# Cross attention: heads masked in the softmax reciprocals on GpSimd, four heads summed on VectorE, one output product per tile

## What is computed

```python
x = x + L1_xattn(layernorm(x), ctx, ctx, mask, padding, Wq, Wk, Wv, Wo)

def L1_xattn(q, k, v, attn_mask, key_padding_mask, Wq, Wk, Wv, Wo):
    qh = (q @ Wq.T) split in 16 heads of 8;  kh = (k @ Wk.T) ...;  vh = (v @ Wv.T) ...
    qh, kh = apply_rope(qh), apply_rope(kh)
    scores = qh @ kh.T / sqrt(8) + masks
    out = softmax(scores) @ vh        # 257 keys
    return (out with its heads side by side) @ Wo.T
```

## Time and profile before

| | us |
|---|---|
| median of three runs | 2311.27 (2311.0 to 2311.86) |
| profiled execution | 2309.65, of which the span is 2307.9 |
| cross attention, first to last `exp` (L2276) | about 1044.5 to 1655.4 in the span |
| one tile in its steady part (four units) | 19.09 |
| PE, DVE, ACT, POOL busy in such a tile | 18.75, 15.54, 14.75, 11.43 |

### The profile page before, as it was taken

The page is one execution under the profiler, slowest core; times in us unless marked ns, Lnnn a source line. Parts: engine busy times, 40 slices in busy tenths (PEclk is TensorE's granted clock), DMA queues, the critical chain, the costliest instruction groups (busy, mean ns, idle before and its releaser), DMA issues. The chain is left out here.

```text
span 2307.9 us, 81023 instructions
## 1 busy us (share of the span) xinstructions
PE 2119.3 (92%) x27948; PEld 1563.2 (68%) x27949; DVE 1535.6 (67%) x5463; ACT 1300.8 (56%) x3747; POOL 1027.1 (45%) x935
## 2 busy tenths in 40 slices
PE   7989999997999899978999999999889999989994
PEld 4657777774677677756777777777556665665992
DVE  4578888874777743347888888888666666754442
ACT  3555555555888433336777777777645555532330
POOL 1024444333888300006555656555266666625115
PEclk9999999997999899988999999999999999979997
DMA  6640000000000000000111111111140000001112
GB/s 161 174 130 1 0 0 0 0 1 1 1 0 0 1 1 0 0 26 25 36 34 34 34 34 34 34 34 34 35 169 0 0 0 0 0 2 41 42 42 77
DMA packets 41208, 71.52 MB, mean 31 GB/s; under 512 B 6176, under 2 KB 30624, under 8 KB 40480
## 3 DMA queue, kind: packets, MB, share of 16 engines
q1 hardware_dynamic: 37792, 63.55, 9.4%
q0 software_dynamic: 3328, 6.82, 0.9%
HBM read 60.91 MB, written 9.44 MB: 30 GB/s over the span
## 5 line engine op out<-in xcount | busy, mean ns | idle before, releaser
L2276 ACT ACTIVATE xat_scores<-xat_scores,xat_least 128x257 f32<-128x257 f32 x512 | 258.5, 505 | 103.5 <-DVE xat_least L2410 102.3
L2410 DVE CUSTOM_DVE_ANT_0 xat_scores<-bank,xat_mask_b 128x257 f32<-128x257 f32 x512 | 207.6, 422 | 88.7 <-PE bank L2120 87.9
L1050 POOL TENSOR_TENSOR gqa_rnorm<-gqa_norm_min,gqa_minus_half 128x12 f32<-128x12 f32 x64 | 145.8, 2278 | 104.9 <-DVE gqa_norm_min L1127 104.9
L2178 PE MATMUL bank<-ident,xat_scores 128*128 128x128 f32 x1024 | 189.2, 287 | 0.0
L2178 PEld LDWEIGHTS bank<-ident,xat_scores 128*128 128x128 f32 x1024 | 116.4, 142 | 81.0 <-issue 49.0
L690 POOL TENSOR_TENSOR lin_q_softmax<-lin_q_exp,lin_q_rsum 128x512 f32<-128x512 f32 x64 | 66.7, 1042 | 223.2 <-DVE lin_q_rsum L751 223.2
L1693 DVE SCALAR_TENSOR_TENSOR X<-bank,expert_shares,X 128x128 f32 (+1 forms) x256 | 72.0, 343 | 130.9 <-PE bank L1607 130.7
L1630 ACT ACTIVATE moe_gelu<-bank 128x512 f32<-128x512 f32 x128 | 76.5, 597 | 146.1 <-PE bank L1597 146.1
L1607 PEld LDWEIGHTS bank<-moe_w,moe_gelu 128*128 128x128 f32 x1024 | 124.2, 192 | 30.8 <-issue 18.2
L1368 POOL TENSOR_TENSOR bat_scores<-bat_scores,bat_max 128x512 f32<-128x512 f32 x128 | 130.5, 1041 | 32.5 <-DVE bat_max L1400 32.5
L1400 DVE CUSTOM_DVE_ANT_0 bat_scores<-bank,bat_causal_add 128x128 f32<-128x128 f32 x512 | 110.7, 286 | 47.2 <-PE bank L1256 47.2
(11 more groups left out here) (320 smaller groups left out, 5826.9 us busy)
## 6 DMA issues: line engine op xcount, KB each, us to landing
glu_ctx_N<-in_ctxN SPq DMA_DIRECT2D x32, 576.0 KB, 4.3
xat_ctx_T<-in_ctxT SPq DMA_DIRECT2D x32, 516.0 KB, 3.6
xat_pad<-in_xat_pad SPq DMA_DIRECT2D x32, 128.5 KB, 3.4
expert_w<-in_glx_w SPq DMA_DIRECT2D x1, 4096.0 KB, 14.9
slot_rows<-gqa_zero_rows SPq DMA_DIRECT2D x1, 2560.0 KB, 11.0
slt_rows<-slot_rows SPq DMA_DIRECT2D x40, 64.0 KB, 1.8
slot_results<-slt_y POOLq DMA_DIRECT2D x40, 64.0 KB, 1.8
moe_w<-in_moe_w SPq DMA_DIRECT2D x2, 1024.0 KB, 5.8
```

The costliest lines, as they stand in the source:

```text
L1050: pool.tensor_tensor(rn[h][:, :], sm[h][:, :], half_neg[:, :], ALU.pow).then_inc(rnorm, 1)
L2178: m = pe.transpose(dst[:, c * P:(c + 1) * P], sx[j % 2][:, g, c * P:(c + 1) * P], k.ident[:, :])
L2276: act.activation(sx[j % 2][:, g, :], sx[j % 2][:, g, :], ACT.Exp, bias=mn[j % 2][g][:, 0:1], scale=-1.0, accum_out=sm[j % 2][:, g:g + 1]). ...
L2410: dve.tensor_tensor_reduce(sx[j % 2][:, g, :], pS[g][:, 0:J], mb[slot][:, j, :], 1.0, BIG, ALU.add, ALU.min, mn[j % 2][g][:, 0:1]).then_in ...
```

## The change

The head mask moves from the output weights to the reciprocals. A new constant `head_of_row` (128x32) is 1 where a row's head group matches the column's head. GpSimd in place of ACT widens the reciprocals (`spread_r` for `r_copy`) and multiplies them by it, so that the transposed reciprocals are zero at the features that belong to another head. DVE's `o_keep` becomes `o_scale`, of the same shape, written in place; a new DVE instruction per unit, `o_sum`, adds the four head columns, 128x128 to 128x32, into a tile `o` of a quarter of the size. `y` is then one product with the plain weights. GpSimd's run for the next tile is cut in pieces between its four `spread_r`. PE's waits for banks are on the new semaphore `o_scaled`; `y` still waits for `o_kept`, which `o_sum` now raises.

```diff
-        woh = sb("w_out_of_head", [P, QH, P])
-        os_ = [sb(f"o{i}", [P, QH, BT, S]) for i in range(2)]
+        os_ = [sb(f"o{i}", [P, BT, S]) for i in range(2)]
@@ PE, y
-                for h in range(QH):
-                    m = pe.matmul(dst[:, 0:P], os_[slot][:, h, :, :], woh[:, h, :], start=(h == 0), stop=(h == QH - 1))
-                m.then_inc(y_made, 1)
+                pe.matmul(dst[:, 0:P], os_[slot][:, :, :], wo[:, :], start=True, stop=True).then_inc(y_made, 1)
@@ PE, body: waits for a bank
-                    pe.wait_ge(wo_ready, QH)
-                        wait(pe, o_kept, u - 1)
+                        wait(pe, o_scaled, u - 1)
@@ ACT, body
-                    if more:
-                        r_copy(*two)
@@ GpSimd
+            def spread_r(t, slot, j):
+                u = BT * t + j
+                pool.wait_ge(recip, u + 1)
+                wait(pool, no_made, u - 1)
+                pool.tensor_tensor(rw[j % 2][:, :, :], spread(rs[j % 2][:, :], 32),
+                                   hrow[:, :].unsqueeze(1).broadcast_to([P, G, 32]), ALU.mult).then_inc(r_spread, 1)
-                if not last:
-                    read_pad(t + 1, 1 - slot)
-                    keep_mask(t + 1, 1 - slot)
-                    add_mask(t + 1, 1 - slot)
-                    keep_ctx(t + 1, 1 - slot)
-                    rotate_q(t + 1)
-                    spread_q(t + 1, 1 - slot)
+                for j in range(BT):
+                    if not (first and j < 2):
+                        spread_r(*ago(t, slot, j, 2))
+                    if j == 0 and not last:
+                        read_pad(t + 1, 1 - slot)
+                    if j == 1 and not last:
+                        keep_mask(t + 1, 1 - slot)
+                        add_mask(t + 1, 1 - slot)
+                    if j == 2 and not last:
+                        keep_ctx(t + 1, 1 - slot)
+                    if j == 3 and not last:
+                        rotate_q(t + 1)
+                        spread_q(t + 1, 1 - slot)
+                if last:
+                    spread_r(t, slot, 2)
+                    spread_r(t, slot, 3)
@@ DVE
-            def o_keep(t, slot, j, at):
+            def o_scale(t, slot, j, at):
                 u = BT * t + j
                 dve.wait_ge(o_mixed, u + 1)
+                dve.tensor_tensor(om[j % 2][:, :, :], om[j % 2][:, :, :],
+                                  unit_bank(*at)[:, RC].rearrange("p (h q) -> p h q", q=S), ALU.mult).then_inc(o_scaled, 1)
+
+            def o_sum(t, slot, j):
+                u = BT * t + j
+                dve.wait_ge(o_scaled, u + 1)
                 wait(dve, y_made, t - 1)
-                dve.tensor_tensor(os_[slot][:, :, j, :], om[j % 2][:, :, :],
-                                  unit_bank(*at)[:, RC].rearrange("p (h q) -> p h q", q=S), ALU.mult).then_inc(o_kept, 1)
+                dve.tensor_reduce(os_[slot][:, j, :], om[j % 2][:, :, :].rearrange("p h q -> p q h"), AX,
+                                  ALU.add).then_inc(o_kept, 1)
@@ DVE, body
-                    for h in range(QH):
-                        dve.tensor_scalar(woh[:, h, :], wo[:, :], hdiag[:, h:h + 1], None, ALU.mult).then_inc(wo_ready, 1)
                         reciprocal(*one)
+                    if more:
+                        o_sum(*two)
                     if j == 0 and not last:
                         norm(t + 1, 1 - slot)
```

More of the change, by code:

```diff
@@ L2030, in sem @@
             return sems[-1]
-        wq, wqr, wk, wv, wo, qtab, cosk, sink, hdiag, mask = preloaded
-        woh = sb("w_out_of_head", [P, QH, P])
+        wq, wqr, wk, wv, wo, qtab, cosk, sink, hdiag, mask, hrow = preloaded
         nmask = sb("mask_negated", [P, J])
@@ L2061, in stage_cross_attention @@
         VC, PC, LC = slice(0, NC * P), slice(NC * P, (NC + 1) * P), slice((NC + 1) * P, (NC + 1) * P + BT)
[L2063 removed]
+        next_loaded, o_scaled = sem("next_weights_loaded"), sem("o_scaled")
         landed = [sem("ctx_landed0"), sem("ctx_landed1")]
@@ L2196, in body @@
                         if j == 1:
-                            wait(pe, o_kept, u - 2)
+                            wait(pe, o_scaled, u - 2)
                         else:
@@ L2226, in body @@
                     if j == 1 and not last:
-                        wait(pe, o_kept, u - 1)
+                        wait(pe, o_scaled, u - 1)
                         x_transpose(t + 1, 1 - slot, (j, XX))
                     if j == 2 and not last:
-                        wait(pe, o_kept, u - 1)
+                        wait(pe, o_scaled, u - 1)
                         q(t + 1, 1 - slot, (j, XX))
                     if j == 3 and not first:
-                        pe.wait_ge(o_kept, u - 1)
+                        pe.wait_ge(o_scaled, u - 1)
                         y(t - 1, 1 - slot, (j, XX))
@@ L2277, in exp @@
                                accum_out=sm[j % 2][:, g:g + 1]).then_inc(s_exp, 1)
-            def r_copy(t, slot, j):
-                u = BT * t + j
-                act.wait_ge(recip, u + 1)
-                wait(act, no_made, u - 1)
-                act.activation(rw[j % 2][:, :, :], spread(rs[j % 2][:, :], 32), ACT.Copy).then_inc(r_spread, 1)
             def p_copy(t, slot, j):
@@ L2300, in body @@
                 for j in range(BT):
-                    some, more = not (first and j == 0), not (first and j < 2)
-                    one, two = ago(t, slot, j, 1), ago(t, slot, j, 2)
-                    if more:
-                        r_copy(*two)
+                    some = not (first and j == 0)
+                    one = ago(t, slot, j, 1)
                     if some:
@@ L2477, in body @@
                     if more:
-                        o_keep(*two, (j, NO))
+                        o_scale(*two, (j, NO))
                     least(t, slot, j, 3)
@@ L2491, in body @@
                     o_mix(t, slot, 2, (0, NO))
-                    o_keep(t, slot, 2, (0, NO))
+                    o_scale(t, slot, 2, (0, NO))
                     t_copy(t, slot, 3, 3, (0, T3))
                     reciprocal(t, slot, 3)
+                    o_sum(t, slot, 2)
                     aggregate(dve, k, added, 2 * NT - 2, 0, NT - 1)
                     o_mix(t, slot, 3, (0, XX))
-                    o_keep(t, slot, 3, (0, XX))
+                    o_scale(t, slot, 3, (0, XX))
+                    o_sum(t, slot, 3)
                     add(t, (1, T1))
@@ L2537, in build @@
                 ("q_table", [P, 2, 2 * P]), ("cos_k", [P, J]), ("sin_k", [P, J]), ("head_in_group", [P, 4]),
-                ("mask", [P, J]))]
+                ("mask", [P, J]), ("head_of_row", [P, 32]))]
             for_linear = [(lin[0][:, :, :, :], a["lin_wqkv"]), (lin[1][:, :, :], a["lin_wout"]),
@@ L2546, in build @@
             for_cross = [(t[tuple(slice(None) for _ in t.shape)], a["xat_" + n]) for t, n in zip(
-                xat, ("wq", "wq_rot", "wk", "wv", "wo", "q_table", "cos_k", "sin_k", "head_in_group", "mask"))]
+                xat, ("wq", "wq_rot", "wk", "wv", "wo", "q_table", "cos_k", "sin_k", "head_in_group", "mask", "head_of_row"))]
             for_clamped = [(t[tuple(slice(None) for _ in t.shape)], a[n]) for t, n in zip(
@@ L2651, in layouts @@
     o["xat_head_in_group"] = ((row[:, None] % 32) // 8 == np.arange(4)[None]).astype(np.float32)
+    o["xat_head_of_row"] = (row[:, None] // 32 == np.arange(32)[None] // 8).astype(np.float32)
     o["xat_mask"] = np.tile(g["mask_1x1xSxS2_fk0"].reshape(S, J), (4, 1))
```

3 lines of the change are left out of this document (removed).

## The result

The kernel after takes 2289.70 us (median of 4 runs, 2286.35 to 2290.88), the kernel before 2311.14 in the same comparison (2309.11 to 2311.86). The ratio is 0.9911, 95% interval 0.9897 to 0.9924. The forecast was 2288.3, in a range of 2284 to 2300. The profiled execution after took 2290.58 with a span of 2288.1 (before 2309.65 and 2307.9); the mean granted TensorE clock was 0.968 in it, 0.966 before.

What follows compares the result with a forecast made beforehand. PE was taken as the bound, with `y` lengthening each fourth unit. 30 x 0.73 = 21.9 us plus 0.25 and 0.8 gave 22.95 us gained, 2286.7 profiled and 2288.3 as median, range 2284 to 2300.

Steps and rivals of the forecast that it cites:

- The mechanism: End of each tile's fourth unit: eight passes of `y` hold PE 1.08 us and delay the next scores.
- y, 0.73 per tile: Fourth unit on PE: cutting `y` from eight passes to two saves 0.73 us per tile, 5.23 to 4.50.
- the loop that was to take over at 4.50: Scores, DVE's run from first to fourth `least`, then the next scores: 4.50 us a unit with nothing in between.
- o_sum: New DVE reduction in each unit: 0.28 us, hidden in DVE's wait for the scores with 0.21 us slack, cost nothing.
- spread_r: GpSimd's widening of reciprocals: 0.48 us, third unit's ready at S + 1.78 (S: scores' start), wanted at 2.12, cost nothing.
- rival B: Third unit's late `spread_r` stops PE and decides the tile; slower beyond a cost c of 1.0, 2328 at 1.27; chance 0.07.
- Contention: DVE's normalization beside GpSimd's `spread_r` in every second unit: nothing at its median; worst case 1.04 us, 0.19 per tile.
- rival A: `spread_r` at 0.73 us or the normalization's worst case, 6 us each: 2294 for one, 2300 for both; chance 0.13.
- Start and end: Stage's start 0; at its end the last `y` gains 0.8 us and the `y` before it 0.25.
- The total: Whole kernel: 22.95 us gained, profiled execution 2309.65 to 2286.7, median of the runs 1.62 above it, 2288.3.
- C: Scores behind `y` were held by DVE's masks all along, so a shorter `y` gives nothing: 2311; chance 0.03.
- rest of 0.02: Chance left for outcomes beyond the range, beside the rivals of a slower kernel and of no difference.

Runs made afterwards that it cites:

- e1_y_four: The kernel after with its one output product issued four times, so eight passes as before: 2308.56 us, ratio 0.9991 to the kernel before.
- before_y_one: The kernel before with only the first of its four output products (three heads left out), nothing else changed: 2290.04 us, ratio 0.9907.
- spread_x2: The kernel after with one more GpSimd product of the same shape ahead of each `spread_r`: 2292.47 us, ratio 0.9917 to the kernel before.
- spread_x3: The kernel after with two more GpSimd products of the same shape ahead of each `spread_r`, on another chip: ratio 0.9997 to the kernel before.
- e5_before_pe_loop4: The kernel before with PE's loop body written out over four tiles instead of two: 2335.72 us, ratio 1.0104 to the kernel before.
- sum_x3: The kernel after with two more VectorE reductions of the same shape ahead of each `o_sum`: 2392.02 us, ratio 1.0347 to the kernel before.

## Why the prediction was right

**The mechanism.** `y` in the way of the scores, and nothing else: right, by e1_y_four and before_y_one from both sides. That the total came so near is partly luck (below).

**y, 0.73 per tile: the term that was too large.** Two parts of it failed. The step "PE is free at 1310.86 to 1310.92, before the masks allow the next scores" priced two passes at 0.27 to 0.33. Measured from the start of `y` to the start of the scores they hold PE 0.42, which is 0.13 behind the last `least`'s result instead of 0.06, and the fourth unit is 4.57 and not 4.50. A price per pass taken from eight queued ones (1.08 / 8 = 0.135) spreads over all of them the 0.19 us that stays when passes go; with 0.11 a pass and that share, two make 0.42. (The other price, 0.33 from the four passes of `q`, is 0.32 by its own row, and has the same fault.) So PE, and not the masks, still lets the scores go: from eight passes to four and to two the unit fell by the same 0.11 a pass, and the loop that was to take over at 4.50 had not done so. And a unit's end was treated as the same everywhere, while every second one has PE's turn behind `y`: 4.84. From the first scores of the stage to those of its last unit it is 609.05 before and 592.18 after, -16.87 for the forecast -21.9. Of the missing 5.0 the 13 turns at 0.33 short of 0.73 make 4.3, and the other 17 tiles, at 0.07 on average, make 1.2 (0.5 comes back in the other units by hundredths). The warning was in the code and in the trace, though not in the rows shown: PE's body of two tiles, and first units of 4.63 beside 4.50 in the kernel before, where VectorE's first `least` comes 1.57 us behind the scores instead of 1.42.

**o_sum.** Forecast 0.28, recorded 0.345 and 0.26 to 0.27 to the next instruction's start. The slack in the first unit was forecast as 0.21 and stands in the trace as 0.22 away from the turn. Hidden, as said.

**spread_r.** Forecast 0.48 with bounds 0.45 to 0.73; recorded 0.40, 0.36 from start to start, below the lower bound. The reciprocal of the second unit ended at S + 0.37, as forecast. The third unit's product is ready at S + 1.34 instead of 1.78; of the 0.44, two products cheaper than 0.48 make half, and the steps between instructions, priced at about 0.1 each where the record has overlaps, the other half. That leaves 0.78 us of slack for 0.34. The point from which rival B decides was put at c = 1.0; spread_x2 (0.8) costs nothing, and spread_x3 (1.2) lies a little beyond the point.

**Contention.** Median 389 ns and longest 882, for 558 and 1037 before: not worse, as taken, but not for the reason given. The prediction took the duration as a spread. It follows a rule that all fourteen traces of this case show: in 31 of the 32 tiles (25 in e5_before_pe_loop4) the normalization starts while a GpSimd instruction runs, and each time it ends 0.08 to 0.09 us behind that one's end. A GpSimd instruction that starts while it runs does not lengthen it. In the kernel before it starts near the end of the second mask instruction (1314.59 + 2.38 = 1316.97; 1316.45 + 0.60 = 1317.05):

```profile
1316.45 0.60 DVE L2386 TENSOR_SCALAR xat_xn<-X,mean_var,rstd 128x128 f32 x1
```

In the kernel after it starts at 1309.36, behind the start of the short `spread_r` (1309.27 to 1309.67), and is done at 1309.75, though the mask instruction has begun at 1309.63. In sum_x3 it starts behind the mask instruction and waits for all of it, and the second unit grows by 1.5 us, where the reductions were to cost 0.2. The worst case of 1.04 that rival A priced at 0.19 us a tile is in before_y_one, where the median is 1.08 and the longest 1.27: there the second units are 4.54 to 4.58 in all but one of the steady tiles, at most 0.04 longer.

**Start and end.** From the stage's table load to its first scores 14.22 before and 13.86 after (forecast 0); from the last unit's scores to the next stage's load 13.81 and 13.14, so -0.67 for the forecast -1.05. The last output product waits as it did in the earlier trace rows, for `o_sum` now (timeline of the kernel after):

```profile
1645.31 0.80 PE L2168 MATMUL bank<-xat_w_out,xat_o 128*128 128x128 f32 x2 [1.87 <-DVE xat_o L2447]
```

**The total.** The stage brought 17.9 us of the forecast 22.95. That the median still came within 1.4 us of the forecast is owed partly to the stage behind it, which happened to be 2.7 us shorter in the profiled execution, and to the spread of a few us between runs. That is luck. The same mechanism with its true sizes gives 2309.65 - 17.9 + 1.6 = 2293.4 from the profile of before; the runs of before_y_one and of the kernel after, at 2290, lie a little below that.

**The rivals.** A did not come (its GpSimd half needs 0.73, it was 0.40; its other half is worth 0.04 a tile at most). B did not come and would have from somewhat below 1.2 us on. C is refuted by the units. (The chances of the forecast and the rivals add up to 1, so the "rest of 0.02" had no room beside them.)

## What to carry to other kernels

Look at which instruction stands between a unit and the next unit's first product, and at which loop takes over once it is short; a sum over blocks of zeros is paid in TensorE passes there, while the same sum on an engine that waits anyway is free. But the passes that go had a second job: they kept TensorE busy while its sequencer turned the loop. Before adding work to a hidden place, look beyond the wait in front of it, at what the shift does to the order of a VectorE and a GpSimd instruction on SBUF, and at the length of the loop body.

## What the runs showed of the hardware

- A loop's turn on PE: behind an output product of two or of four passes, the scores start 0.7 us behind its start. With two that is 0.20 us without work at the scores and 0.27 us in the unit, with four it is 0.06, with eight nothing in that unit, though 0.08 us in the next one hang on it. The Trainium skill ("Advanced Engine Details and Errata", section "Control Flow Timing") gives about 51 ns for a branch and 108 ns for a compare and branch. The trace shows a gap of 200 ns; what in it is the branch and what the registers and waits behind it, no row tells apart.
- A few passes between two waits do not cost in proportion: 0.42 us for two, 0.64 for four, 1.09 for eight, which is 0.19 and 0.11 a pass.
- A body that has become too long is brought again at every turn: PE, four tiles instead of two, 3.3 us of standstill at the turn shown and about 0.15 MB each time; VectorE, 16 more instructions than in a body that was still held, 3.09 us and about 0.04 MB.
- The normalization, a `tensor_scalar` of VectorE from SBUF to SBUF of 0.35 us, ends 0.08 us behind the GpSimd instruction in which it started: 1.98 us in all when that one is a two-operand instruction of 2.2 us. The `least`, with an operand in a bank, stayed at 0.42 beside it, and the 128x128 reduction from SBUF at 0.37.
- The stage behind the cross attention took 380.0 to 385.4 us with unchanged code, and the last stage 298 to 301 us on one chip for 259 to 261 on the others. Neither is explained here.
